# POOL's head products in halves: the order of products and masks in a four-layer kernel

## Chip, cores and metric

One core of one Trainium2 chip. The metric is the device time of one run of the whole kernel, in microseconds (us), the median of several runs.

## The reference, cut to what matters

The kernel computes four layers (an attention and a feed-forward part each) on 16 sequences of 512 tokens with 128 features. Two of the eight parts matter here.

Part 5, rotary causal attention with 16 heads of 8 features:

```python
q = _rope(proj(Wq, bq), e)
k = _rope(proj(Wk, bk), e)
v = proj(Wv, bv)
att = jnp.einsum('bhqd,bhkd->bhqk', q, k) / scale
att = jnp.where(causal[None, None], att, -jnp.inf)
att = jax.nn.softmax(att, axis=-1)
y = jnp.einsum('bhqk,bhkd->bhqd', att, v)
```

Part 8, where every token attends over its own 16 heads, before a small mixture of experts:

```python
att = jnp.einsum('bthd,btgd->bthg', q, k) / np.sqrt(HD)
att = jax.nn.softmax(att, axis=-1)
out = jnp.einsum('bthg,btgd->bthd', att, v).reshape(b, t, D)
```

For each token and each pair of heads these are 8 multiplications and a sum; POOL multiplies and VectorE sums.

## The kernel before

**Passes.** Sequences are worked on in pairs (index q, 0 or 1). A first part takes parts 1 to 4 of the reference pair by pair, then all experts of part 4 are run, then a loop of eight passes takes parts 5 to 8 (layers 4 to 7 in the code). The head attention and experts of part 8 of one pair are not done at the end of a pass: they are interleaved with part 5 and 6 of the next pass. A last part (`first == LAYERS`, once) finishes the last pair alone.

**Head products.** For a pair there are 16 products, m = 0 to 15: m 0 to 7 are phase 0 (queries by keys, four tiles of 128 tokens for each q), m 8 to 15 phase 1 (exponents by values). POOL writes product m, 128 partitions by 16 x 16 x 8 = 2,048 elements, into `ht_pr[m % 2]` (line 766), and VectorE sums over the innermost axis in two instructions of eight heads each, `take(m, 0)` and `take(m, 1)` (lines 1483 and 1486). Before product m, from m = 2 on, POOL waits for `f_read` at m - 1, which take(m - 2, 1) raises. Before take(m, half), VectorE waits for `f_pool` at m + 1.

**Part 5.** It goes over 8 quartets of heads, c = 0 to 7, each in six steps u = 0 to 5. A step has two heads and a part of the 4 x 4 tiles: steps 0 and 1 are 512 wide, 2 and 3 384, 4 and 5 256 and 128. Each engine runs its list in program order, for c from -2 to 8 and u from 0 to 5:

- TensorE: `scores_t(c, u)` (line 1909), `scores(c + 2, u)` (line 1891), then at u = 0 `values(c - 1, 1)`, at u = 1 `turn_max(c + 1)` and `values(c - 1, 2)`, at u = 3 `spread_sums(c - 1)` (line 1991), at u = 4 `values(c, 0)` (line 1932). `values(c, b)` waits for the masks of steps 2b and 2b + 1 of quartet c. Scores go round three PSUM buffers, each waiting for its reader of three turns before.
- VectorE: `maxima(c + 2, u)` on the scores (line 919), a take where `TAKE_STEP` has one, the head maxima (lines 1496 and 1497), sums (1503, 1504) or outputs (1509) at u = 1 of quartets 2 to 6 and 8, `shift(c + 1)` at u = 1 (line 943), `divide(c - 1)` at u = 5 (line 935).
- ScalarE: the exponents of `scores_t(c, u)` (line 1554), which go round five buffers.
- POOL: `mask(c, u)` on the exponents (lines 712 and 716), and between them the products: product 2 + 2c after mask (c, 1), product 3 + 2c after mask (c, 5), for c = 0 to 6. Products 0 and 1 come before quartet 0.

The takes stand at (c + 1, 0) and (c + 1, 2) for product 2 + 2c, and at (c + 1, 4) and (c + 1, 5) for product 3 + 2c. So the buffer of product 2 + 2c becomes free at VectorE's step (c, 2), that of product 3 + 2c at step (c, 5). There are two buffers.

Of the kernel before, what the change touches and what calls it, by code (L numbers as in the profile page):

```python
# [28 lines left out]
P = 128  # L29
NT = T // P  # L30
PAIR = (0, 1)
H = 16
DH = D // H
# [22 lines left out]
def program(nc, dram, x_in, out, sorted_x, sorted_y, kept_x, routes, returns, starts):  # L56
    with ExitStack() as ctx:
# [348 lines left out]
        for first, last in PARTS:  # L406
            if first == L1_EXPERTS + 1:
                sg = Signals()
# [243 lines left out]
            with nc.Fori(0, SEQS // 2 if first < LAYERS else 1) as pair:  # L652
                sg = Signals()
                with nc.Block(no_gpsimd_drain=True) as block:
# [47 lines left out]
                    def _(pool):  # L702
# [43 lines left out]
                                    if 0 <= c < QUARTETS and u % 3 == 1:  # L746
                                        send_rows(pool, sg, (2 * QUARTETS + 2 * c + u // 3,))

                        def product(m):

                            phase, q, t = m // (2 * NT), m // NT % 2, m % NT
                            if m >= 2:
                                pool.wait_ge(sg["f_read"], m - 1)
                            kv = ht_kv[q][:, t]
                            if phase == 0:
                                pr = ht_pr[m % 2].rearrange("p (h g d) -> p h g d", h=H, g=H)
                                left = ht_q[q][:, t].rearrange("p (h d) -> p h d", h=H).unsqueeze(2)
                                right = kv[:, 0:D].rearrange("p (g d) -> p g d", g=H).unsqueeze(1)
                                shape = [P, H, H, DH]
                            else:  # L760
                                pool.wait_ge(sg["f_exp"], q + 1)
                                pr = ht_pr[m % 2].rearrange("p (h d g) -> p h d g", h=H, d=DH)
                                left = ht_sc[q][:, t].unsqueeze(2)
                                right = kv[:, D:2 * D].rearrange("p (g d) -> p d g", g=H).unsqueeze(1)
                                shape = [P, H, DH, H]
                            pool.tensor_tensor(pr, left.broadcast_to(shape), right.broadcast_to(shape),  # L766
                                               ALU.mult).then_inc(sg["f_pool"], 1)

                        def finish_norms():
# [12 lines left out]
                        def l2_masks():  # L782
                            for c in range(QUARTETS):
                                for u in range(STEPS_OF):
                                    mask("l2", c, u)
                                    if u == 1 and c < HEAD_QUARTETS:
                                        product(2 + 2 * c)
                                if c < HEAD_QUARTETS:
                                    product(3 + 2 * c)

                        if first == L2_ATTENTION:
                            l2_clear()
                        if first == LAYERS:
                            for m in range(4 * NT):
                                product(m)
                            finish_norms()
                        n = 0
                        for layer in range(first, min(last, LAYERS)):
# [41 lines left out]
                            if layer == L2_ATTENTION:  # L840
                                pool.wait_ge(sg["l2_v"], len(PAIR))
                                for m in range(2):
                                    product(m)
                                l2_masks()
                            if layer == L2_ATTENTION + 1:
                                finish_norms()
# [12 lines left out]
                    def _(dve):  # L859
# [314 lines left out]
                        def l2_attention():  # L1174
# [13 lines left out]
                            def beside(c, u):  # L1188
                                if (c, u) in TAKE_STEP:
                                    take(*TAKE_STEP[c, u])  # L1190
                                if (c, u) == (2, 1):
# [285 lines left out]
                        def take(m, half):  # L1477

                            phase, q, t = m // (2 * NT), m // NT % 2, m % NT
                            dve.wait_ge(sg["f_pool"], m + 1)  # L1480
                            heads = slice(H // 2 * half, H // 2 * (half + 1))
                            if phase == 0:
                                i = dve.tensor_reduce(ht_sc[q][:, t, heads], ht_pr[m % 2].rearrange(  # L1483
                                    "p (h g d) -> p h g d", h=H, g=H)[:, heads], AX, ALU.add)
                            else:
                                i = dve.tensor_reduce(ht_o[q][:, t].rearrange("p (h d) -> p h d", h=H)[:, heads],  # L1486
                                                      ht_pr[m % 2].rearrange("p (h d g) -> p h d g", h=H, d=DH)[:, heads],
                                                      AX, ALU.add)
                            if half == 1:
                                i.then_inc(sg["f_read"], 1)  # L1490
# [1047 lines left out]
EXPERT_PAIRS = 4  # L2538
BUSY = 6
HEAD_QUARTETS = 7  # L2540
TAKE_STEP = {(-1, 1): (0, 0), (-1, 2): (0, 1), (-1, 4): (1, 0), (0, 0): (1, 1)}
for c_ in range(HEAD_QUARTETS):
    TAKE_STEP[c_ + 1, 0], TAKE_STEP[c_ + 1, 2] = (2 + 2 * c_, 0), (2 + 2 * c_, 1)
    TAKE_STEP[c_ + 1, 4], TAKE_STEP[c_ + 1, 5] = (3 + 2 * c_, 0), (3 + 2 * c_, 1)
KV_BANK = ((2, 3), (6, 7))
# [159 lines left out]
```

## Time and profile before

| | |
|---|---|
| median of 3 runs | 5653.43 us (5645.69 to 5659.54) |
| profiled execution | 5696.46 us |
| its span, first to last instruction | 5694.9 us |
| mean granted TensorE clock | 0.858 of full speed |
| instructions | 86289 |
| products on POOL (line 766) | 144: 16 in each of 8 passes and in the last part |

The profile is of one execution. A group of rows gives the busy time of the instructions of a line and the mean or median of one; a timeline row gives the start, the busy time, and in brackets how long the engine had been idle before it and which instruction released it. "x4" at the end of a timeline row means that it merges four instructions. `w_mo_wgu` in the rows is the store that holds `ht_pr`, `ht_sc` and one of the key and value buffers; `spare` and `absorbed_q` hold queries, and later outputs, of q = 0 and 1.

### The profile page before, as it was taken

The page shows a single profiled execution, that of the slowest core. Times are in us where ns is not written, and L with a number is a line of the kernel's source. Part 1 is how long each engine was busy: PE and PEld are TensorE (multiplying, and loading weights), DVE is VectorE, ACT ScalarE, POOL GpSimd, SP SyncE. Part 2 cuts the span into 40 slices and gives each one's busy share as a digit, 9 for nine tenths or more (in the row PEclk, how much of TensorE's full clock was granted, in tenths as well). Part 3 has the DMA queues.
Part 4 walks back from the last instruction along what each step waited for, and adds up shares of the span by engine and source line. Part 5 has one row for each costly group of instructions (what it writes and reads, how often), then busy time and mean ns, then how long its engine had stood idle before and what let it go on. Part 6 is the DMA issues. An engine that isn't in the chain of part 4 may idle for free. (4 is left out here: it accounts for less than half of the span.)

```text
span 5694.9 us, 86289 instructions
## 1 busy us (share of the span) xinstructions
PE 4378.5 (77%) x31912; PEld 2428.5 (43%) x31912; DVE 3661.7 (64%) x10829; ACT 1786.3 (31%) x2787; POOL 2281.8 (40%) x2766
## 2 busy tenths in 40 slices
PE   6969797888879796776778778687787886877872
PEld 4444444454535453443343443434443434344341
DVE  4565656565556565458677686685776866768765
ACT  2424242423333323333224232332232422423230
POOL 3333332323333333556336244372362533624435
PEclk9989898989989898887878888888788888888885
DMA  3000000000000001760000000000000000000000
GB/s 122 11 15 16 9 16 9 16 9 16 9 16 10 15 10 57 226 188 14 14 16 7 17 10 9 14 9 17 14 6 18 9 10 17 9 17 11 9 14 4
DMA packets 143893, 147.30 MB, mean 26 GB/s; under 512 B 31180, under 2 KB 128142, under 8 KB 142926
## 3 DMA queue, kind: packets, MB, share of 16 engines
q1 hardware_dynamic: 116286, 94.67, 5.6%
q0 software_dynamic: 18432, 37.79, 2.3%
q10 hardware_dynamic: 8736, 8.91, 0.5%
q8 instruction: 285, 4.67, 0.3%
q14 instruction: 154, 1.26, 0.1%
HBM read 70.83 MB, written 63.11 MB: 24 GB/s over the span
## 5 line engine op out<-in xcount | busy, mean ns | idle before, releaser
L919 DVE CUSTOM_DVE_ANT_0 twin<-twin,w_mask_row 128x512 f32<-128x512 f32 (+3 forms) x2048 | 950.9, 520 | 333.1 <-PE twin L1891 331.4
L1891 PE MATMUL twin<-arena 32*128 32x128 f32 (+3 forms) x4096 | 809.4, 522 | 37.0 <-DVE arena L919 16.9
L1909 PE MATMUL twin<-arena 32*128 32x128 f32 (+3 forms) x4096 | 795.9, 507 | 31.1 <-DVE arena L919 29.7
L1554 ACT ACTIVATE arena<-twin 128x768 f32<-128x768 f32 (+1 forms) x544 | 478.9, 880 | 674.4 <-PE twin L1920 387.9
L1909 PEld LDWEIGHTS twin<-arena 32*128 32x128 f32 x4096 | 351.9, 202 | 482.0 <-issue 293.6
L827 POOL TENSOR_SCALAR ve<-mv 128x4 f32<-128x4 f32 x128 | 27.5, 215 | 1158.2 <-DVE mv L879 1157.5
L377 POOL DMA_INDIRECT got<-sorted_y,back x288 | 278.1, 966 | 495.7 <-ACT ring L1758 306.2
L1836 PE MATMUL twin<-w_ident_b 128*128 128x512 bf16 x1200 | 344.5, 438 | 132.3 <-DVE mv L879 50.3
L1891 PEld LDWEIGHTS twin<-arena 32*128 32x128 f32 x4096 | 361.0, 208 | 196.2 <-issue 109.0
L369 POOL DMA_INDIRECT sorted_x<-got,w_mo_first_slots x288 | 284.1, 986 | 139.7 <-issue 65.5
L1932 PE MATMUL twin<-arena 128*32 128x128 f32 (+3 forms) x2944 | 304.1, 457 | 9.0 <-POOL arena L712 9.0
L919 DVE DVE_READ_ACCUMULATOR2_ANT arena<- 128x1 f32 x2048 | 288.8, 141 | 0.0
L712 POOL TENSOR_SCALAR_AFFINE_SELECT arena<-arena 128x256 f32<-128x256 f32 x352 | 144.7, 413 | 345.0 <-ACT arena L1554 344.5
L1554 ACT ACTIVATE ring<-twin 128x768 f32<-128x768 f32 (+1 forms) x224 | 194.9, 878 | 218.8 <-PE twin L1909 216.9
L1836 PEld LDWEIGHTS twin<-w_ident_b 128*128 128x128 bf16 x1200 | 121.2, 110 | 330.6 <-DVE mv L879 69.5
L833 POOL TENSOR_TENSOR rs<-ve,minus_half 128x4 f32<-128x4 f32 x208 | 223.3, 1073 | 17.3
L766 POOL TENSOR_TENSOR w_mo_wgu<-w_mo_wgu,w_l_cs_feat 128x2048 f32<-128x2048 f32 x36 | 197.4, 5488 | 52.5 <-DVE w_mo_wgu L1483 25.6
L1932 PE MATMUL twin<-ring,arena 128*32 128x384 f32 (+3 forms) x1152 | 163.1, 525 | 57.3 <-POOL ring L712 50.0
L766 POOL TENSOR_TENSOR w_mo_wgu<-w_mo_wgu 128x2048 f32<-128x2048 f32 x36 | 197.7, 5495 | 20.0 <-DVE spare L1486 14.1
L766 POOL TENSOR_TENSOR w_mo_wgu<-spare,w_l_cs_feat 128x2048 f32<-128x2048 f32 x36 | 161.4, 4495 | 88.8 <-DVE arena L1183 85.9
L716 POOL TENSOR_SCALAR_AFFINE_SELECT arena<-arena 128x512 f32<-128x512 f32 x192 | 123.8, 650 | 160.0 <-ACT arena L1554 159.9
L1483 DVE TENSOR_REDUCE w_mo_wgu<-w_mo_wgu 128x128 f32<-128x1024 f32 x144 | 174.1, 1214 | 20.8 <-POOL w_mo_wgu L766 20.8
(440 smaller groups left out, 9392.6 us busy)
## 6 DMA issues: line engine op xcount, KB each, us to landing
sorted_y<-arena SPq DMA_DIRECT2D x96, 256.0 KB, 2.8
sorted_x<-zeros ACTq DMA_DIRECT2D x2, 4096.0 KB, 20.0
a<-sorted_x SPq DMA_DIRECT2D x64, 128.0 KB, 2.5
b<-sorted_x SPq DMA_DIRECT2D x64, 128.0 KB, 3.0
hres<-sorted_x SPq DMA_DIRECT2D x64, 128.0 KB, 2.5
x<-x_in SPq DMA_DIRECT2D x18, 256.0 KB, 3.4
sorted_x<-got,w_mo_first_slots POOLq DMA_INDIRECT x288
x_next<-kept_x SPq DMA_DIRECT2D x18, 256.0 KB, 2.8
```

Of the source, the lines that this page charges most:

```text
L369: pool.indirect_dma_start(sorted_x[r % GROUPS], bass.IndirectOffsetOnAxis(ap=slot_of[:, q, n:n + 1], axis=0), normed[q][:, r // GROUPS], N ...
L377: pool.indirect_dma_start(got[q][:, n], None, sorted_y, bass.IndirectOffsetOnAxis(ap=back[:, q, n:n + 1].bitcast(U32), axis=0)).then_inc(s ...
L712: pool.affine_select(p, p, [[0, 2], [1, P]], ALU.is_ge, 0.0, base=0, channel_multiplier=-1).then_inc(sg[tag + "_masked"], 1)
L766: pool.tensor_tensor(pr, left.broadcast_to(shape), right.broadcast_to(shape), ALU.mult).then_inc(sg["f_pool"], 1)
L833: pool.tensor_tensor(RS[q][:], VE[q][:], minus_half[:], ALU.pow).then_inc(sg["rstd_ready"], 1)
L919: last = dve.tensor_tensor_reduce(s[:, e, at:at + w], s[:, e, at:at + w], W["mask_row"][:, T - w:T], -1.0, 3e38, ALU.add, ALU.min, into)
L1483: i = dve.tensor_reduce(ht_sc[q][:, t, heads], ht_pr[m % 2].rearrange("p (h g d) -> p h g d", h=H, g=H)[:, heads], AX, ALU.add)
L1554: act.activation(at_pt[tag][n % len(at_pt[tag])][:, :, 0:w], twin[SLOT["scores_t", c, u] % 3][:, :, 0:w], ACT.Exp, scale=1.0 if tag == "l1 ...
L1836: pe.matmul(into, ident_b, ident_b.unsqueeze(1).broadcast_to([P, NT, P]), start=True, stop=True, skip_group_check=True)
L1891: last = pe.matmul(s[:, e, at:at + w], queries[r, P * i:P * (i + 1)], keys[r, 0:w], start=(at == 0), stop=True, skip_group_check=True)
L1909: last = pe.matmul(s[:, e, at:at + w], keys[r, P * m:P * (m + 1)], queries[r, P * m:T], start=(at == 0), stop=(tag == "l2"), skip_group_ch ...
L1932: last = pe.matmul(bank[into][rows_of(j), P * m:T], weights(m, j), at_pt[tag][n % len(at_pt[tag])][:, j % 2, at:at + w], start=(m == 0), s ...
```

## The change

Each product becomes two instructions of eight heads, 1,024 elements each, both behind the same wait for `f_read`, and each raises `f_pool`. A take waits for its own half. In part 5 the four halves of a quartet stand behind the masks of steps 0, 1, 3 and 5 (`HALF_AT`), where the two whole products stood behind those of steps 1 and 5. In the last part, and for products 0 and 1, the two halves follow each other.

```diff
-                        def product(m):
+                        def product(m, half):
                             phase, q, t = m // (2 * NT), m // NT % 2, m % NT
+                            heads = slice(H // 2 * half, H // 2 * (half + 1))
                             if m >= 2:
                                 pool.wait_ge(sg["f_read"], m - 1)
...
-                                shape = [P, H, H, DH]
+                                shape = [P, H // 2, H, DH]
...
-                            pool.tensor_tensor(pr, left.broadcast_to(shape), right.broadcast_to(shape),
+                            pool.tensor_tensor(pr[:, heads], left[:, heads].broadcast_to(shape), right.broadcast_to(shape),
                                                ALU.mult).then_inc(sg["f_pool"], 1)
...
                                 for u in range(STEPS_OF):
                                     mask("l2", c, u)
-                                    if u == 1 and c < HEAD_QUARTETS:
-                                        product(2 + 2 * c)
-                                if c < HEAD_QUARTETS:
-                                    product(3 + 2 * c)
+                                    if c < HEAD_QUARTETS and u in HALF_AT:
+                                        which, half = divmod(HALF_AT.index(u), 2)
+                                        product(2 + 2 * c + which, half)
...
-                            dve.wait_ge(sg["f_pool"], m + 1)
+                            dve.wait_ge(sg["f_pool"], 2 * m + half + 1)
...
+HALF_AT = (0, 1, 3, 5)
```

## Rows read from the trace of the kernel before

**Rows 1.** The page: busy time of each engine over the span

```profile
PE 4378.5 (77%) x31912; PEld 2428.5 (43%) x31912; DVE 3661.7 (64%) x10829; ACT 1786.3 (31%) x2787; POOL 2281.8 (40%) x2766
```

**Rows 2.** Timeline of POOL, first pass, last pass: start, us, [idle before, releaser]

```profile
2635.16 4.52 POOL L766 TENSOR_TENSOR w_mo_wgu<-absorbed_q,w_mo_wgu 128x2048 f32<-128x2048 f32 x1 [1.93 <-DVE w_mo_wgu L1483]
...
2645.99 0.80 POOL L712 TENSOR_SCALAR_AFFINE_SELECT ring<-ring 128x256 f32<-128x256 f32 x2
2650.76 4.51 POOL L766 TENSOR_TENSOR w_mo_wgu<-absorbed_q,w_mo_wgu 128x2048 f32<-128x2048 f32 x1 [3.97 <-DVE w_mo_wgu L1483]
...
2655.94 0.65 POOL L716 TENSOR_SCALAR_AFFINE_SELECT arena<-arena 128x512 f32<-128x512 f32 x1
...
2657.14 4.54 POOL L766 TENSOR_TENSOR w_mo_wgu<-absorbed_q,w_mo_wgu 128x2048 f32<-128x2048 f32 x1
...
2665.87 5.44 POOL L766 TENSOR_TENSOR w_mo_wgu<-w_mo_wgu,w_l_cs_feat 128x2048 f32<-128x2048 f32 x1 [3.47 <-DVE w_mo_wgu L1483]
...
2682.55 5.47 POOL L766 TENSOR_TENSOR w_mo_wgu<-w_mo_wgu,w_l_cs_feat 128x2048 f32<-128x2048 f32 x1 [2.18 <-DVE spare L1486]
...
2697.51 5.46 POOL L766 TENSOR_TENSOR w_mo_wgu<-w_mo_wgu 128x2048 f32<-128x2048 f32 x1 [1.42 <-DVE spare L1486]
...
2719.92 5.49 POOL L766 TENSOR_TENSOR w_mo_wgu<-w_mo_wgu 128x2048 f32<-128x2048 f32 x1
...
5238.23 4.51 POOL L766 TENSOR_TENSOR w_mo_wgu<-absorbed_q,w_mo_wgu 128x2048 f32<-128x2048 f32 x1 [1.93 <-DVE w_mo_wgu L1483]
...
5300.05 5.43 POOL L766 TENSOR_TENSOR w_mo_wgu<-w_mo_wgu 128x2048 f32<-128x2048 f32 x1 [1.22 <-DVE spare L1486]
```

**Rows 3.** Timeline of VectorE, first pass

```profile
2640.11 1.21 DVE L1483 TENSOR_REDUCE w_mo_wgu<-w_mo_wgu 128x128 f32<-128x1024 f32 x1
...
2646.73 1.23 DVE L1497 TENSOR_TENSOR w_mo_wgu<-w_mo_wgu 128x1024 f32<-128x1024 f32 x1
...
2649.46 1.22 DVE L1483 TENSOR_REDUCE w_mo_wgu<-w_mo_wgu 128x128 f32<-128x1024 f32 x1
...
2652.19 0.43 DVE L919 CUSTOM_DVE_ANT_0 twin<-twin,w_mask_row 128x256 f32<-128x256 f32 x1 [0.47 <-PE twin L1891]
...
2654.55 0.42 DVE L919 CUSTOM_DVE_ANT_0 twin<-twin,w_mask_row 128x256 f32<-128x256 f32 x1
...
2655.77 1.21 DVE L1483 TENSOR_REDUCE w_mo_wgu<-w_mo_wgu 128x128 f32<-128x1024 f32 x1
...
2664.57 1.21 DVE L1483 TENSOR_REDUCE w_mo_wgu<-w_mo_wgu 128x128 f32<-128x1024 f32 x1
...
2670.30 1.22 DVE L1483 TENSOR_REDUCE w_mo_wgu<-w_mo_wgu 128x128 f32<-128x1024 f32 x1
...
2704.82 6.00 DVE L1509 TENSOR_TENSOR spare<-spare,w_mo_wgu 128x512 f32<-128x512 f32 x1
```

**Rows 4.** Timeline of TensorE, first pass

```profile
2652.01 1.19 PE L1932 MATMUL twin<-ring,arena 128*32 128x512 f32 x8
2653.13 0.48 PE L1909 MATMUL twin<-arena 32*128 32x256 f32 x2
...
2665.67 1.07 PE L1932 MATMUL twin<-ring,arena 128*32 128x512 f32 x8
...
2672.09 0.86 PE L1932 MATMUL twin<-arena 128*32 128x384 f32 x8 [2.15 <-POOL arena L712]
...
2703.76 1.51 PE L1932 MATMUL twin<-ring,arena 128*32 128x384 f32 x8 [2.57 <-POOL ring L712]
```

**Rows 5.** Line 1932, all passes: TensorE's idle time until this row's instruction: us, times

```profile
  POOL ring L712: 125.3, 61
```

**Rows 6.** Timeline of POOL in layer 0: a 1,024-element product

```profile
61.00 2.37 POOL L802 TENSOR_TENSOR w_mo_wgu<-w_mo_wgu,w_l_cs_feat 128x1024 f32<-128x1024 f32 x1
```

**Rows 7.** Line 1509 over the span: min/median/max ns

```profile
L1509 DVE TENSOR_TENSOR spare<-spare,w_mo_wgu x9: 674/5552/6011, 2704.8 to 5625.4; 128x512 f32<-128x512 f32 x9
```

**Rows 8.** Windows, quartet 5: PE, PEld, DVE, ACT, POOL busy, clock, DMA share, GB/s

```profile
2697.50:2712.50 15.00, 11.81 (x86) 4.71 (x86) 15.00 (x28) 6.78 (x9) 13.94 (x8) 0.77 0.00 1
```

More of the change, by code:

```diff
@@ L764, in product @@
                                 right = kv[:, D:2 * D].rearrange("p (g d) -> p d g", g=H).unsqueeze(1)
-                                shape = [P, H, DH, H]
-                            pool.tensor_tensor(pr, left.broadcast_to(shape), right.broadcast_to(shape),
+                                shape = [P, H // 2, DH, H]
+                            pool.tensor_tensor(pr[:, heads], left[:, heads].broadcast_to(shape), right.broadcast_to(shape),
                                                ALU.mult).then_inc(sg["f_pool"], 1)
@@ L794, in _ @@
                             for m in range(4 * NT):
-                                product(m)
+                                product(m, 0)
+                                product(m, 1)
                             finish_norms()
@@ L842, in _ @@
                                 for m in range(2):
-                                    product(m)
+                                    product(m, 0)
+                                    product(m, 1)
                                 l2_masks()
```

## The prediction

> **What bounds the kernel now.** I read the page first [rows 1]: TensorE is busy 77% of the span, VectorE 64%, POOL 40%. No engine is full on average, so the stage has to be looked at alone. The change touches one stage: the attention of layer 4 with the head products of the last layer interleaved into it, once in each of eight passes, and again the products alone in the last part. There I read the timelines of POOL, VectorE and TensorE side by side, with quartets c and steps u as in the kernel section. Write T(c) for the end of the reduction (the "take") at step (c, 2), U(c) for the end of the one at step (c, 5).
>
> The reader is to see three things. VectorE runs almost without a gap: from T(2) = 2650.68 to T(3) = 2665.78 its one gap is 0.47 us, before the maxima at 2652.19 [rows 3]. POOL has room, but not in every place: product 2+2c starts 0.08 us after T(c), having waited 3.97, 3.47, 2.18 and 1.42 us for it [rows 2]. Both masks (c, 0) and (c, 1) had been made before that wait (the pair at 2645.99) [rows 2]. And TensorE takes the masked tiles in program order: `values` (c, 0) at 2652.01 in quartet 2 and at 2665.67 in quartet 3, thus 1.3 us after T(2) and 0.1 us before T(3), without an idle bracket, since its masks were long there. Where POOL's long product does stand in TensorE's way is `values` (c, 1): 2.15 and 2.57 us idle until the mask, 125.3 us over all passes [rows 4, 5].
>
> **What the change does, part by part.** The buffer a product writes is free at the same event as before: its wait is `f_read` at m - 1, which the second half of a take raises. So half products don't start earlier than T(c) and U(c). What moves is what is queued behind the wait on POOL. Product (2+2c, 0) now stands ahead of mask (c, 1), and product (3+2c, 0) ahead of masks (c, 4) and (c, 5). The masks now wait for T(c), or U(c), and then for a half product. POOL sends no DMA here and SP's queue isn't passed.
>
> Price of a half: the trace has a 128x1024 product of POOL, 2.37 us [rows 6], against 4.51 for 2,048 elements [rows 2], so halving leaves about 0.12 us behind on each half. For the slower form of phase 1 I take 5.46 / 2 + 0.1 = 2.83. (Lower bound: exactly half, 2.25 and 2.73.)
>
> **New first part, T(c) to U(c).** 0.08 until the half starts, 2.37 the half, 0.40 the mask (c, 1), 0.06 to TensorE, 1.12 `values` (c, 0) (2652.01 to 2653.13), 0.95 the two score groups of step 5 (2653.13 to 2654.08), 0.12 to VectorE, 1.22 its maxima (2654.55 to 2655.77), 1.21 the take: 7.53 us, in phase 1 (c from 3) 7.99. Before it was 6.30 in quartet 2 (2650.68 to 2656.98) and 5.74 in quartet 3 (2665.78 to 2671.52) [rows 2, 3, 4]. TensorE had been ahead of VectorE by only 0.5 us in quartet 2 (scores done 2654.08, maxima at 2654.55), so this is not swallowed.
>
> **New second part, U(c) to T(c+1).** POOL: half, masks (c, 4) and (c, 5) (0.65 + 0.60), then the other half. TensorE gets mask (c, 5) at U + 3.7 to 4.2 and has the scores of step (c+1, 2) done 1.8 us later, at U + 6; VectorE comes to them only at U + 6.6 or later. So this part stays VectorE's own: 8.80 us after an even quartet (2656.98 to 2665.78) and 9.36 after an odd one (2641.32 to 2650.68) [rows 3]. One thing is added. The DVE product 128x1024 of line 1497 begins 5.41 us after U(1) (2646.73), and in the new order POOL's other half then runs, until U + 6.07 in phase 0 and U + 6.99 in phase 1. The trace shows what comes of that: line 1509, the same kind of instruction on 128x512, took 6.00 us at 2704.82 (POOL's product 13 began at the same moment), with a median of 5.55 against a least of 0.67 [rows 3, 7]. It was held until POOL's instruction ended. That would add 0.66 us in quartet 1 and 1.58 in quartet 3.
>
> That row has a rule in the Trainium skill, page "SBUF — State Buffer", section "Who interferes with whom": a DVE instruction with two inputs in SBUF and a GpSimd one that reads SBUF share a read port, and whichever starts first holds it to its end. The trace agrees (6.00 us for what takes 0.67 alone). By itself the rule speaks for the change: shorter POOL instructions hold VectorE for less.
>
> **Sum of a pass.** T(1) to T(5): quartet 1: 7.53 + 9.36 + 0.66 = 17.55; 2: 7.53 + 8.80 = 16.33; 3: 7.99 + 9.36 + 1.58 = 18.93; 4: 7.99 + 8.80 = 16.79; together 69.6 us. Before: 62.35 (2635.16 to 2697.51), in the last pass 61.82 [rows 2], over the eight passes 61.82 to 63.86 with mean 62.7. So +6.9. Quartet 0 has no wait for a take on these products and is left as it is.
> Tail, from T(5) on: VectorE has no maxima after quartet 5 and POOL alone paces. New: 7.99 to U(5), 0.08, then six halves (13 to 15) of 2.83 and masks of 0.4 + 0.4 + 0.8 + 1.25 + 1.25 = 4.1: 29.15 us. Before: 2697.51 to 2725.41, 27.9 [rows 2]; over the passes 26.7 to 27.95, mean 27.4. So +1.7. The held head output (6.00 us) gets shorter, but POOL's 1.2 us wait behind it was already all that it cost. What follows the tail (masks and values of quartet 7, the outputs) is serial and moves along.
> Together +8.6 us a pass. Whether line 1497 is really held depends on a phase of one or two us, so I count half of the 2.24: +7.5, times eight +60. In the last part 16 products run back to back on POOL (four in 21.79 us): 32 halves cost some 0.1 us more each product, +1.6, and two takes overlap a half, -2.4: -1. **+59 us.**
>
> The profiled execution took 5696.46 us (span 5694.9), the median of the runs is 5653.43, 43 below; its stages are taken as those of any run, so I add the same 59 to the median: **5712 us**.
>
> Bounds. Low: halves at exactly half (8 on the path and 6 in the tail, -1.6 a pass) and line 1497 never held (-2.24): +4.75 a pass, 38 - 1 = +37, 5690. High: line 1497 held in full (8.6) and TensorE's clock low. The windows of quartet 5 show 0.77 granted, and after 2.57 us idle the eight 384-wide matmuls took 1.51 us where they had taken 0.86 in quartet 3: towards the lower of the two levels, 1.2 GHz, after an idle wait [rows 4, 8]. The new order makes a wait of 2 to 3 us ahead of `values` (c, 0). At the low clock the 1.12 + 0.95 cost 1.85 more, in four quartets 7.4: 16 us a pass, +128, 5781.
>
> The Trainium skill says, in "TensorE: Matmul & The Clock Gate", section "Part 1: The HAM clock gate", that an idle engine falls to 1.2 GHz and must be busy again to get 2.4. The trace shows both levels in this very stage; by that rule the sum goes towards its upper bound.
>
> **Rivals.**
> *Faster.* Product and mask finely interleaved: `values` (c, 1) no longer waits (2.15 us in quartet 3), the head output is held for half as long. What VectorE could get back is U(3) to T(4), 10.95 us against the 9.36 of its own work = 1.6, about 0.5 in quartet 4, and POOL's 1.2 in the tail: 3.3 a pass, -26: 5627. It decides if mask (c, 1) isn't late, that is if TensorE arrives at `values` (c, 0) more than 2.9 us after T(c). It arrived 1.3 after and 0.1 before, so I give it little.
> *No change.* TensorE's delay lies in VectorE's shadow and only the tail's overhead stays: 5650 to 5665. It needs scores ready over 2 us before their maxima at step 5; they were 0.5 us ahead.
> *Clock.* As the upper bound: TensorE low in most quartets, 5781 or a little above.
>
> **How the numbers follow.** Forecast (5685 to 5755) 0.60; clock and other additions above it 0.11; a smaller loss, 5670 to 5685, 0.09; no change 0.10; faster 0.10. The 0.3% that a measurement of this kernel can tell from no change is 17 us. Slower 0.80, same 0.10, faster 0.10. For 8 in 10 the range reaches down to 5648 and up to 5780; the likeliest case's own range is 5685 to 5755.
>
> **What would show it.** Right: TensorE's idle until a mask moves from `values` (c, 1) to `values` (c, 0), 2 to 3 us each; T(1) to T(5) grows to about 69 us; VectorE idles 1 to 2 us before the maxima of step 5; half products at 2.3 to 2.4 and 2.8 us; line 1509 falls below 4 us and line 1497 rises above 1.23. Wrong: TensorE reaches `values` (c, 0) later than I think, or VectorE's gap is filled by work it had put off; then the quartets keep their 15 to 17 us.

## The result and the profile after

The changed kernel takes 5752.97 us (median of 4 runs, 5747.67 to 5753.94), the kernel before 5651.65 us on the same chip (4 runs): ratio 1.0178, 95% interval 1.0159 to 1.0197, or 101 us slower. The profiled execution took 5752.96 us, its span 5751.4 us, mean clock 0.855.

The page of the changed kernel, busy time and VectorE's maxima (last column: VectorE's idle time ahead of the group and what ended it):

```profile
PE 4380.7 (76%) x31912; PEld 2422.8 (42%) x31912; DVE 3664.8 (64%) x10829; ACT 1784.6 (31%) x2787; POOL 2318.1 (40%) x2910
...
L921 DVE CUSTOM_DVE_ANT_0 twin<-twin,w_mask_row 128x512 f32<-128x512 f32 (+3 forms) x2048 | 950.2, 519 | 422.2 <-PE twin L1893 421.0
```

VectorE and TensorE are busy as long as before, POOL 36.3 us longer for 144 more instructions [rows 1]. So nearly all of the loss is waiting, and the page already says where: VectorE waits 421 us for scores of line 1893 (that group had 331.4 us in the page of before). The timelines show how. POOL, quartets 2 and 3 of the first pass:

```profile
2599.82 2.33 POOL L767 TENSOR_TENSOR w_mo_wgu<-absorbed_q,w_mo_wgu 128x1024 f32<-128x1024 f32 x1 [2.54 <-DVE w_mo_wgu L1485]
2602.10 0.40 POOL L712 TENSOR_SCALAR_AFFINE_SELECT ring<-ring 128x256 f32<-128x256 f32 x1
2602.48 2.34 POOL L767 TENSOR_TENSOR w_mo_wgu<-absorbed_q,w_mo_wgu 128x1024 f32<-128x1024 f32 x1
...
2617.08 2.79 POOL L767 TENSOR_TENSOR w_mo_wgu<-w_mo_wgu,w_l_cs_feat 128x1024 f32<-128x1024 f32 x1 [2.59 <-DVE w_mo_wgu L1485]
2619.81 0.42 POOL L712 TENSOR_SCALAR_AFFINE_SELECT ring<-ring 128x256 f32<-128x256 f32 x1
2620.19 2.84 POOL L767 TENSOR_TENSOR w_mo_wgu<-w_mo_wgu,w_l_cs_feat 128x1024 f32<-128x1024 f32 x1
...
2626.41 2.82 POOL L767 TENSOR_TENSOR w_mo_wgu<-w_mo_wgu,w_l_cs_feat 128x1024 f32<-128x1024 f32 x1 [2.65 <-DVE w_mo_wgu L1485]
```

TensorE, the same places:

```profile
2602.55 1.48 PE L1934 MATMUL twin<-ring,arena 128*32 128x512 f32 x8 [2.87 <-POOL ring L712]
...
2620.28 1.94 PE L1934 MATMUL twin<-ring,arena 128*32 128x512 f32 x8 [2.95 <-POOL ring L712]
2622.15 0.80 PE L1911 MATMUL twin<-arena 32*128 32x256 f32 x2
```

And VectorE:

```profile
2619.17 1.21 DVE L1485 TENSOR_REDUCE w_mo_wgu<-w_mo_wgu 128x128 f32<-128x1024 f32 x1
2623.88 0.43 DVE L921 CUSTOM_DVE_ANT_0 twin<-twin,w_mask_row 128x256 f32<-128x256 f32 x1 [3.50 <-PE twin L1893]
...
2625.11 1.21 DVE L1485 TENSOR_REDUCE w_mo_wgu<-w_mo_wgu 128x128 f32<-128x1024 f32 x1
```

The reader is to follow one round. POOL waits for the take that frees the buffer until 2617.08. Mask (3, 1) is queued behind that half product: it is done at 2620.23. TensorE has waited 2.95 us for it and begins `values` (3, 0) at 2620.28. The scores of step 5 are queued behind `values`, so VectorE idles 3.50 us before its maxima at 2623.88, and only then comes the next take, whose end at 2626.32 frees the buffer for the next product at 2626.41. In the kernel before, the same `values` had no idle bracket [rows 4], and VectorE's one gap in a quartet was 0.47 us [rows 3].

All waits of TensorE's matmuls of line 1934 for a mask, over the eight passes (us, times):

```profile
  POOL ring L712: 74.9, 41
  POOL arena L716: 54.3, 24
  POOL ring L716: 37.2, 23
  POOL arena L712: 31.0, 14
```

Together 197.4 us, against 65.7 us in the kernel before, 50.0 of it in the first group. The 125.3 us of [rows 5] is larger because that view adds the idle time ahead of the weight loads of the same line, which is largely the same time: it would count a wait twice.

For the rest I use one measure for all kernels, read from the starts of the products in the POOL timeline: T(1) to T(5) is the time from the start of product 4 to that of product 12, the tail from there to the end of product 15, the pass is from product 0 to the end of product 15 (means over eight passes); "last part" is the same from product 0 to the end of product 15 there. With more than two buffers a product no longer starts at the end of a take, and there only the column "pass" compares. "Masks" is the sum of the matmuls' waits as above. "Held" is the time by which VectorE's 16 subtractions of the head maxima (two in each pass, line 1499, 1.23 us when nothing holds them) took longer than that. All but the ratio is read from the one profiled execution of each kernel.

| kernel | ratio to before, 95% | T(1) to T(5) | tail | pass | last part | masks | held |
|---|---|---|---|---|---|---|---|
| before | 1 | 62.70 | 27.46 | 130.3 | 85.54 | 65.7 | 6.8 |
| changed | 1.0178 (1.0159 to 1.0197) | 72.71 | 29.19 | 142.0 | 90.96 | 197.4 | 13.7 |
| split only | 0.999 (0.997 to 1.001) | 63.27 | 27.26 | 131.3 | 86.68 | 85.9 | 12.3 |
| whole early | 1.0524 (1.0496 to 1.0552) | 91.3 | 31.1 | 161.9 | 85.53 | 277.7 | 2.3 |
| early first | 1.0153 (1.0132 to 1.0174) | 72.62 | 28.94 | 142.4 | 86.76 | 136.2 | 0.7 |
| early second | 1.0069 (1.0051 to 1.0088) | 64.58 | 28.13 | 132.5 | 90.98 | 130.1 | 12.1 |
| filled | 1.0171 (1.0132 to 1.0211) | 68.83 | 29.97 | 138.3 | 86.72 | 139.5 | 13.8 |
| three buffers | 0.9983 (0.9968 to 0.9998) | 64.17 | 29.0 | 128.5 | 91.02 | 33.1 | 29.2 |
| three buffers, whole | 1.005 (1.0036 to 1.0063) | 68.6 | 28.62 | 134.3 | 85.59 | 23.6 | 58.8 |
| four buffers | 1.0047 (1.0027 to 1.0067) | 65.54 | 29.75 | 130.9 | 86.18 | 26.9 | 44.0 |
| four buffers, whole | 1.009 (1.0071 to 1.0108) | 67.25 | 27.03 | 133.2 | 85.06 | 23.6 | 57.0 |
| before, no subtraction | 0.995 (0.993 to 0.9969) | 58.68 | 27.91 | 127.4 | 83.25 | 82.9 | - |
| changed, no subtraction | 1.0119 (1.0102 to 1.0136) | 67.33 | 29.48 | 137.7 | 84.46 | 169.1 | - |
| four, no subtraction | 0.9851 (0.9831 to 0.9872) | 54.01 | 30.32 | 119.3 | 83.96 | 17.5 | - |

A pass grew by 11.7 us: 8 x 11.7 = 93.6, and 5.4 in the last part, 99 us. This is not quite the whole: from the start of the first product to the end of the span the trace of the changed kernel is 109 us longer than that of before (3208.2 against 3099.2). Some 11 us lie between the passes (241.5 us from a product 15 to the next product 0, against 240.1), a stretch that wasn't followed; without whole early, the other kernels have 239.0 to 242.1 there. The medians differ by 101, so a sum from these two traces is good to some 10 us. The runs stood on several chips, and the median of the kernel before was 5645 to 5652 us on some and 5689 to 5693 on others, a difference that lies ahead of the eight passes. That is why ratios are taken within a chip, and why the profile of before (5696.46 us) stands 43 us above its median: its first product starts at 2595.7, that of the changed kernel at 2543.2.

### The profile page after: what moved, and what is told of

Read it like the earlier page. It is cut to its first block and busy times, and to the rows that moved or that the text cites. A ratio compares the mean times of both kernels' runs of the same rounds, so it can differ in the third digit from the quotient of the medians.

```text
span 5751.4 us, 86505 instructions
## 1 busy us (share of the span) xinstructions
PE 4380.7 (76%) x31912; PEld 2422.8 (42%) x31912; DVE 3664.8 (64%) x10829; ACT 1784.6 (31%) x2787; POOL 2318.1 (40%) x2910
## 5 line engine op out<-in xcount | busy, mean ns | idle before, releaser
L1893 PE MATMUL twin<-arena 32*128 32x128 f32 (+3 forms) x4096 | 837.4, 537 | 42.5 <-DVE arena L921 18.9
L1911 PE MATMUL twin<-arena 32*128 32x128 f32 (+3 forms) x4096 | 810.3, 521 | 7.9 <-DVE arena L921 6.7
L1911 PEld LDWEIGHTS twin<-arena 32*128 32x128 f32 x4096 | 365.8, 209 | 454.6 <-issue 307.2
L1893 PEld LDWEIGHTS twin<-arena 32*128 32x128 f32 x4096 | 370.0, 213 | 219.2 <-issue 106.2
L1934 PE MATMUL twin<-arena 128*32 128x128 f32 (+3 forms) x2944 | 317.1, 467 | 85.3 <-POOL arena L716 54.3
L767 POOL TENSOR_TENSOR w_mo_wgu<-w_mo_wgu,w_l_cs_feat 128x1024 f32<-128x1024 f32 x72 | 203.5, 2830 | 88.0 <-DVE w_mo_wgu L1485 46.6
L767 POOL TENSOR_TENSOR w_mo_wgu<-w_mo_wgu 128x1024 f32<-128x1024 f32 x72 | 202.5, 2817 | 32.8 <-DVE spare L1488 28.1
L767 POOL TENSOR_TENSOR w_mo_wgu<-absorbed_q,w_mo_wgu 128x1024 f32<-128x1024 f32 x72 | 168.6, 2347 | 89.6 <-DVE w_mo_wgu L1485 89.6
L767 POOL TENSOR_TENSOR w_mo_wgu<-spare,w_l_cs_feat 128x1024 f32<-128x1024 f32 x72 | 166.8, 2334 | 87.4 <-DVE arena L1185 84.5
```

What stands on the lines that cost most here:

```text
L767: pool.tensor_tensor(pr[:, heads], left[:, heads].broadcast_to(shape), right.broadcast_to(shape), ALU.mult).then_inc(sg["f_pool"], 1)
L1893: last = pe.matmul(s[:, e, at:at + w], queries[r, P * i:P * (i + 1)], keys[r, 0:w], start=(at == 0), stop=True, skip_group_check=True)
L1911: last = pe.matmul(s[:, e, at:at + w], keys[r, P * m:P * (m + 1)], queries[r, P * m:T], start=(at == 0), stop=(tag == "l2"), skip_group_ch ...
L1934: last = pe.matmul(bank[into][rows_of(j), P * m:T], weights(m, j), at_pt[tag][n % len(at_pt[tag])][:, j % 2, at:at + w], start=(m == 0), s ...
```

## The experiments

**1. Split only.** The changed kernel, with the halves where the whole products had been.

```diff
-                                    if c < HEAD_QUARTETS and u in HALF_AT:
-                                        which, half = divmod(HALF_AT.index(u), 2)
-                                        product(2 + 2 * c + which, half)
+                                    for n, behind in enumerate(HALF_AT if c < HEAD_QUARTETS else ()):
+                                        if behind == u:
+                                            product(2 + 2 * c + n // 2, n % 2)
-HALF_AT = (0, 1, 3, 5)
+HALF_AT = (1, 1, 5, 5)
```

> Halves as in the changed kernel, but back in the places of the whole products: both halves of product 2+2c behind mask (c, 1), both of 3+2c behind mask (c, 5). Queue theory (the loss comes from masks that stand behind the wait for the buffer): T(1) to T(5) back to 62 to 64 us a pass, the overhead of 0.1 us a half shows only in the tail (+0.6 a pass) and a shorter hold of the head output gives up to 1.2 back; in all 5640 to 5665. Rival (the splitting itself costs, by 144 more POOL instructions, counts and holds of VectorE): 5700 or more.

Measured: 5640.99 us against 5644.58, ratio 0.999 (0.997 to 1.001). The 144 added instructions cost nothing that can be told. The loss is in the places.

**2. Whole early.** The kernel before, with its whole products behind steps 0 and 3.

```diff
-                                    if u == 1 and c < HEAD_QUARTETS:
+                                    if u == 0 and c < HEAD_QUARTETS:
                                         product(2 + 2 * c)
-                                if c < HEAD_QUARTETS:
-                                    product(3 + 2 * c)
+                                    if u == 3 and c < HEAD_QUARTETS:
+                                        product(3 + 2 * c)
```

> The kernel before with whole products, but product 2+2c behind mask (c, 0) and 3+2c behind mask (c, 3): the places of the first halves of the change. Queue theory: mask (c, 1) now waits for T(c) and a whole product, 2.2 to 2.7 us longer than in the changed kernel, and masks (c, 4) and (c, 5) put the values (c, 2) past VectorE's own pace by 1.5 to 2: T(1) to T(5) about 88 us, the kernel 5840 to 5910. Rival (splitting itself costs): close to the kernel before, 5650 to 5680.

Measured: 5945.29 us, ratio 1.0524, T(1) to T(5) 91.3 us, both above what I had written (about 88 us, 5840 to 5910). With the whole product ahead of the masks the chain is a half product longer still. In the first pass TensorE waits 2.34 to 4.45 us ahead of the `values` (c, 0) of quartets 1 to 5.

**3. Three buffers.** The changed kernel with a third product buffer, so that product m waits for the takes of m - 3.

```diff
+        ht_pr.append(got[0][:].rearrange("p n d -> p (n d)"))
...
-                            if m >= 2:
-                                pool.wait_ge(sg["f_read"], m - 1)
+                            if m >= 3:
+                                pool.wait_ge(sg["f_read"], m - 2)
...
-                                pr = ht_pr[m % 2].rearrange("p (h g d) -> p h g d", h=H, g=H)
+                                pr = ht_pr[m % 3].rearrange("p (h g d) -> p h g d", h=H, g=H)
```

> The changed kernel with a third product buffer (in the store of the fetched rows, unused in this stage), so that a half product waits for the take of three products before and finds it done. Order of masks and halves unchanged. Queue theory with the wait for the buffer as its cause: POOL's waits for takes are gone, mask (c, 1) comes about 2.8 us after mask (c, 0) at most, T(1) to T(5) 59 to 63 us a pass, the kernel 5610 to 5655. If instead the fine interleaving as such is at fault (more POOL work ahead of a mask), it stays above 5700.

Measured: 5638.58 us, ratio 0.9983 (0.9968 to 0.9998); a pass takes 128.5 us against 142.0. The order of POOL's queue is that of the change, only the wait at its head is for an earlier take, and the whole loss is gone: TensorE's waits for masks fall from 197.4 to 33.1 us. It is the fastest full kernel of this study, 0.2% below the kernel before, just clear of no difference. T(1) to T(5) is 64.17 us, above the 59 to 63 that I had expected; VectorE's holds, which grow here, stand with experiment 12.

**4. Filled.** The changed kernel, in which TensorE does eight matmuls of 512 columns that nobody reads, in the time in which it would wait for mask (c, 1). They change its activity and nothing that others wait for.

```diff
-                                pe.wait_ge(sg[tag + "_masked"], STEPS_OF * c + 2 * b + 2)
                                 if b == 0 and c >= 1:
                                     pe.wait_ge(sg["l1_y" if tag == "l1" else "l2_taken"], c)
+                                if tag == "l2" and b == 0 and 1 <= c < HEAD_QUARTETS:
+                                    for _ in range(FILL):
+                                        pe.matmul(bank[6], ident_b, ident_b.unsqueeze(1).broadcast_to([P, NT, P]),
+                                                  start=True, stop=True, skip_group_check=True)
+                                pe.wait_ge(sg[tag + "_masked"], STEPS_OF * c + 2 * b + 2)
...
+FILL = 8
```

> The changed kernel with eight bf16 matmuls of 512 columns (results overwritten) in front of values (c, 0), c = 1 to 6, where TensorE idles for 3 us. The mask's wait stays as it is. If the low TensorE clock makes the part that my sum missed (about 1.2 us in quartets 2 to 5), values (c, 0) falls from 1.94 to about 1.1 us, U - T from 9.3 to 8.0 to 8.3, the kernel by 25 to 40 us to 5713 to 5728. If the clock doesn't matter, the time stays at 5753 or rises, as the fill may outlast the wait.

TensorE of this kernel in quartet 3 of the first pass, to be held beside the rows at 2620.28 above:

```profile
2618.61 1.90 PE L1962 MATMUL twin<-w_ident_b 128*128 128x512 bf16 x8
2621.66 1.07 PE L1934 MATMUL twin<-ring,arena 128*32 128x512 f32 x8 [1.15 <-POOL ring L712]
2622.66 0.48 PE L1911 MATMUL twin<-arena 32*128 32x256 f32 x2
```

Its VectorE, the maxima behind them:

```profile
2623.72 0.43 DVE L921 CUSTOM_DVE_ANT_0 twin<-twin,w_mask_row 128x256 f32<-128x256 f32 x1 [1.99 <-PE twin L1893]
```

Windows of the first pass, product 4 to the end of product 15 (PE, PEld, DVE, ACT and POOL busy, clock, DMA share, GB/s), of this kernel:

```profile
2582.70:2685.00 102.30, 82.99 (x612) 33.70 (x612) 81.28 (x199) 43.08 (x56) 80.29 (x59) 0.91 0.00 1
```

and of the changed kernel, then of its quartets 2, 4 and 5 alone:

```profile
2582.70:2685.60 102.90, 76.29 (x559) 31.19 (x558) 79.05 (x193) 41.88 (x54) 81.26 (x60) 0.83 0.00 1
...
2599.80:2617.10 17.30, 12.61 (x102) 5.49 (x102) 14.58 (x41) 6.51 (x9) 11.96 (x11) 0.90 0.00 1
2637.10:2655.30 18.20, 13.04 (x92) 5.19 (x86) 14.56 (x40) 7.31 (x9) 13.81 (x10) 0.78 0.00 0
2655.30:2672.50 17.20, 13.41 (x89) 5.38 (x88) 12.98 (x29) 5.74 (x8) 14.63 (x11) 0.70 0.01 2
```

The same eight matmuls of `values` (3, 0) take 1.07 us with the fill and 1.94 without, 1.07 before [rows 4]; VectorE's gap falls from 3.50 to 1.99 us, T(1) to T(5) from 72.71 to 68.83 us, and the granted clock of the stretch rises from 0.83 to 0.91 (0.89 in the kernel before). The time of the run did not follow beyond doubt: the median was 5736.83 us, ratio 1.0171 (1.0132 to 1.0211), where I had expected 5713 to 5728, and this profiled execution was the fastest of its four, 5707.91 us. What the clock is worth in a pass is thus read from one execution. The four differ in clock as well: those of 5707.91 and 5722.91 us had a mean granted clock of 0.870 and 0.867, those of 5750.75 and 5759.42 us had 0.857 and 0.856, near the 0.852 to 0.855 of the changed kernel. So only two of the four had a higher clock with the fill, and why isn't known. The Trainium skill says in "TensorE: Matmul & The Clock Gate", section "Part 1: The HAM clock gate", that the throttled clock is the default and that activity releases it. This case agrees: activity alone, with nothing done sooner by it, gave 1.07 for 1.94 us.

**5 and 6. Early first, early second.** Only the first, or only the second product's halves where the change puts them. The loop is that of experiment 1.

```diff
-HALF_AT = (0, 1, 3, 5)
+HALF_AT = (0, 1, 5, 5)
```

and for the second

```diff
-HALF_AT = (0, 1, 3, 5)
+HALF_AT = (1, 1, 3, 5)
```

> Halves, with only the first product of a quartet moved forward: product (2+2c, 0) behind mask (c, 0), its other half behind mask (c, 1); both halves of product 3+2c behind mask (c, 5). My point by point account puts the whole loss in this place (the part from T(c) to U(c)): T(1) to T(5) 70 to 73 us a pass, the kernel 65 to 100 us above before, 5710 to 5745. Rival (the delay of masks (c, 4) and (c, 5) is what costs): within 20 us of before.

> Halves, with only the second product moved forward: both halves of product 2+2c behind mask (c, 1), product (3+2c, 0) behind mask (c, 3), its other half behind mask (c, 5). By my account values (c, 2) then wait for masks that come 3.7 to 4.2 us after U(c), but VectorE gets to the scores behind them later still: T(1) to T(5) 63 to 65 us, the kernel within 20 us of before, 5630 to 5665, with a TensorE wait at the values (c, 2) in the trace that costs nothing. Rival: 30 to 60 us slower.

Measured: early first 5777.38 us against 5692.79, ratio 1.0153, a pass 12.1 us longer: as much as in the whole change, and with almost no hold of the subtraction (0.7 us in all). Early second 5725.1 us, ratio 1.0069: 32 us by the medians, 39 by the ratio, outside what I had expected (at most 20). Of these, 8 x 2.2 = 18 us are in the passes and 5.4 in the last part of the profiled execution; some 9 lie between the passes (241.2 us against 240.1), and what they are wasn't followed. Its waits for masks are 130.1 us, nearly those of early first (136.2), and they cost 2.2 us a pass where those cost 12.1: a mask that is late behind U(c) is late in VectorE's shadow, one behind T(c) isn't.

**7 and 8. Four buffers, four buffers whole.** The changed kernel and the kernel before with four product buffers; both edits are as in experiment 3 with 4 for 3.

```diff
+        ht_pr += [got[q][:].rearrange("p n d -> p (n d)") for q in PAIR]
...
+                            if m >= 4:
+                                pool.wait_ge(sg["f_read"], m - 3)
```

> The changed kernel with four product buffers (both stores of fetched rows), so that no half product waits for a take any more; with three, product 3+2c still waited for T(c) and masks (c, 4) and (c, 5) behind it. If the wait for the buffer is the whole cause, POOL never idles for a take, T(1) to T(5) 59 to 63 us and the kernel is 15 to 35 us faster than before, 5610 to 5630. If POOL's work ahead of the masks is a cause of its own, it stays like the three buffers, about 5635.

> The kernel before (whole products in their old places) with four product buffers. Tells what the buffers alone give: POOL no longer idles 1.2 to 4 us before product 2+2c, so masks (c, 2) and (c, 3) come earlier and values (c, 1) don't wait 2 us. If the change's fine spreading has a value of its own once the wait is gone, four_buffers beats this one by 5 us or more; if not, both are the same at 5610 to 5640.

Measured: 5723.57 and 5732.15 us against 5692.79. Both missed: I had expected them below the kernel before, and they are above it, 1.0047 and 1.009. The halves beat the whole products by 9 us, as expected. TensorE's waits for masks are down to 26.9 and 23.6 us, so something else came in. POOL of four buffers, first pass:

```profile
2648.40 2.37 POOL L768 TENSOR_TENSOR got<-absorbed_q,w_mo_wgu 128x1024 f32<-128x1024 f32 x1
2650.68 0.45 POOL L713 TENSOR_SCALAR_AFFINE_SELECT ring<-ring 128x256 f32<-128x256 f32 x1
2651.05 0.45 POOL L713 TENSOR_SCALAR_AFFINE_SELECT arena<-arena 128x256 f32<-128x256 f32 x1
2651.43 2.37 POOL L768 TENSOR_TENSOR got<-absorbed_q,w_mo_wgu 128x1024 f32<-128x1024 f32 x1
2660.13 0.64 POOL L717 TENSOR_SCALAR_AFFINE_SELECT arena<-arena 128x512 f32<-128x512 f32 x1 [6.34 <-ACT arena L1557]
```

VectorE, the same time:

```profile
2648.63 1.21 DVE L1499 TENSOR_REDUCE w_mo_wgu<-w_mo_wgu 128x64 f32<-128x1024 f32 x1
2649.88 5.00 DVE L1500 TENSOR_TENSOR w_mo_wgu<-w_mo_wgu 128x1024 f32<-128x1024 f32 x1
2654.80 0.67 DVE L946 TENSOR_TENSOR arena<-arena,twin 128x512 f32<-128x512 f32 x1
```

The subtraction of the head maxima (two inputs in SBUF, 1.23 us alone) began during a product and ended at 2654.88, over the end of that product, two masks and a whole second product, 1.1 us after POOL had gone idle at 2653.80, which is about its own duration. The first subtraction of each of the eight passes went this way (4.97 to 5.00 us); the second was let in sooner, at the end of a half or shortly behind it (2.63 to 3.74 us). In the changed kernel every hold of a subtraction ended with the half that it had met. VectorE, which bounds the stage, stands meanwhile. The median of these instructions is 4356 ns in four buffers, 4471 in four buffers whole, against 1240 before and 2088 in the changed kernel.

**9 to 11. Without the subtraction.** To measure that, the subtraction is left out in three kernels.

```diff
-                            done(dve.tensor_reduce(red, sc, AX, ALU.max))
-                            dve.tensor_tensor(sc, sc, red.unsqueeze(2).broadcast_to([P, NT * H, H]),
-                                              ALU.subtract).then_inc(sg["f_sc"], 1)
+                            dve.tensor_reduce(red, sc, AX, ALU.max).then_inc(sg["f_sc"], 1)
```

> The kernel before without the subtraction of the head maxima (line 1497, 128x1024, both inputs in SBUF; the exponents are then taken unshifted). It was held by POOL in few passes, so leaving it out saves its own 1.23 us twice a pass where VectorE paces: 10 to 20 us faster than before.

> The changed kernel without the same subtraction. Its hold by POOL's other half was 0.4 and 1.3 us in a pass. If that is the share of the loss that I gave it, this kernel is 14 us closer to its own reference point than before_nosub: 1.2 + 1.7 us a pass less, 25 to 35 us below the changed kernel, and still some 1.2 to 1.5% above before. If the hold is the whole of the loss, it falls to the time of before.

> Four product buffers, halves in the places of the change, without the subtraction. With four buffers POOL runs its products and masks back to back and the subtraction took 4.4 us in the median (up to 5.0) for 1.23. If the hold is what ate the gain of the fourth buffer: 2 times 4.4 us a pass come back, 50 to 75 us below four_buffers, 0.5 to 1% below before and clearly below before_nosub. If something else ate it (POOL's work ahead of the masks), it gains only the 10 to 20 us that before_nosub gains.

Measured: 0.995, 1.0119 and 0.9851. Without it the kernel before wins 0.5 points (28 us, more than the 10 to 20 that I had written), the changed kernel 0.59 points (33 us), that with four buffers 1.96 points (some 110 us, above my 50 to 75). So the hold's share in the loss of the change is about 5 us and can't be told from none; in four buffers the subtraction cost some 110 - 28 = 80 us more than it does in the kernel before, and was what had eaten the gain: without it this kernel is 1.0% faster than the kernel before with the same edit. Of the 80 us the rows show 44.0 - 6.8 = 37 as hold. Where the other half comes from wasn't followed.

**12. Three buffers whole.** The kernel before with the edit of experiment 3.

> The kernel before with a third product buffer, whole products in their old places. Product 2+2c then waits for U(c-1), long past, product 3+2c for T(c). Against three_buffers (0.998 of before): if the spreading in halves is what made that one faster, this is at 1.000 or above; if the third buffer alone did, the same 0.998. With holds of the subtraction by whole products (up to 5.5 us) I expect 1.000 to 1.006.

Measured: 5719.58 us against 5688.84, ratio 1.005 (1.0036 to 1.0063). A third buffer alone is a loss; with the change's order it is none. Halves between masks are thus worth 0.7 points (1.005 against 0.9983) once the wait at their head is gone; whether by the split or by the places, no run tells apart.

The traces point at VectorE's holds. With a third buffer and whole products the 16 subtractions are held for 58.8 us in all (each took 3.85 to 6.17 us), in the kernel before for 6.8; the run is 31 us longer. With halves the holds are 29.2 us. TensorE's waits for masks are no reason: 23.6 us, lower than in the kernel before. This kernel without the subtraction wasn't run, so the cause is argued from rows and not shown.

## Why the prediction was right, and where its sum was short

The forecast was 5712 us, +59; measured was 5752.97, +101, inside the range (5648 to 5780) and just inside the likeliest case's own, which ended at 5755. The mechanism stands; the first part of a round was priced too low, and a term for the last part held in some executions only. This is about them.

**Same start, other queue: right.** Splitting alone does nothing (experiment 1); a third buffer, which moves the wait and not the order, takes the whole loss back (3). Half products of the first pass took 2.33 to 2.38 and 2.79 to 2.86 us (2.37 and 2.83 predicted). The 125.3 us that the prediction gives for TensorE's waits ahead of `values` (c, 1) count weight loads and matmuls both; the matmuls alone waited 50.0 us. The sum didn't use that figure.

**First part, T(c) to U(c): the mechanism right, the size too small.** Predicted 7.53 in phase 0 and 7.99 in phase 1; measured in the first pass 7.3 and 8.5 in quartets 1 and 2 (phase 0), then 9.3, 9.15 and 9.2 in quartets 3 to 5 (phase 1). In quartet 3 the chain is the predicted one link by link to TensorE's start: half from 2617.08 (2.79), mask (0.42), `values` at 2620.28. Then `values` took 1.94 us instead of 1.12, the scores behind it were later by a further 0.6, and VectorE idled 3.50 us, not 1 to 2. I had put TensorE's clock among the rivals with 0.11 and its price at 7.4 us a pass. In the profiled execution with the fill it is 3.9 of the 10.0 us that T(1) to T(5) grew by; the other 6.1 are the queue, for which I had 6.9 less half of the hold, 5.8. In the windows above the granted clock was 0.90 in quartet 2, 0.78 in quartet 4 and 0.70 in quartet 5, where it had been 0.77 [rows 8]. This is the term that failed in the passes: a wait that the change itself brings, once every quartet, lowers the clock of what stands behind it. By how much the run's time would be lower at full clock is less certain than the 3.9, since the four runs of experiment 4 spread over 50 us. The likeliest case's sum had no clock in it, and the result lies only 2 us inside the upper end of that case's range.

**Second part, U(c) to T(c + 1): right.** Predicted 8.80 behind an even quartet, 9.36 behind an odd one, with up to 1.58 for a held subtraction: 10.94 in quartet 3. Measured 8.79, 10.70 and 9.08 in quartets 2, 3 and 4. Experiment 6 shows the same from the other side: the halves behind steps 3 and 5 alone add 2.2 us a pass.

**The held subtraction: half right.** The rows of the 16 subtractions and of the 8 head outputs in the passes of the changed kernel (min/median/max ns):

```profile
L1499 DVE TENSOR_TENSOR w_mo_wgu<-w_mo_wgu x16: 1603/2088/2574, 2595.4 to 5327.2; 128x1024 f32<-128x1024 f32 x16
...
L1511 DVE TENSOR_TENSOR spare<-spare,w_mo_wgu x8: 1791/1802/1810, 2666.1 to 5358.5; 128x512 f32<-128x512 f32 x8
```

Held it was, twice in every pass, for 0.4 us in quartet 1 and 1.3 in quartet 3 (0.66 and 1.58 predicted), and in the passes the head output fell below 4 us as predicted [rows 7]. But in the kernel before the subtraction was held too (up to 2.96 us), so the difference is small: 13.7 us in all against 6.8 by the rows, and 5 us of the 101 by experiments 9 and 10. The passes of early first grow as much as those of the whole change with no hold to speak of.

**Tail: right.** Predicted +1.7, measured 29.19 - 27.46 = +1.73; U(5) to the end of product 15 in the first pass 21.04 us, predicted 21.1.

**Last part: -1 predicted, +5.4 measured in this execution.** VectorE and POOL of the changed kernel there:

```profile
5676.99 10.13 DVE L1511 TENSOR_TENSOR spare<-spare,w_mo_wgu 128x512 f32<-128x512 f32 x1
```

```profile
5675.66 10.92 POOL L767 TENSOR_TENSOR w_mo_wgu<-w_mo_wgu 128x1024 f32<-128x1024 f32 x4
5691.30 10.95 POOL L767 TENSOR_TENSOR w_mo_wgu<-w_mo_wgu 128x1024 f32<-128x1024 f32 x4 [4.72 <-DVE absorbed_q L1488]
```

The head output (0.68 us alone, 3.45 in this place before) was held over the rest of the first half and the three behind it, 10.13 us. The takes behind it came late, POOL ran out of free buffers and waited 4.72 us: that wait is nearly the 5.4. I had priced only the instructions and assumed that a hold ends with the half it met.

Of the 5.4 us, 4 are not the change's own. Split only, early first and filled have the same last part, instruction by instruction. In their profiled executions the same head output was let in behind the first half, took 1.98 to 2.00 us, and the last part took 86.7 to 86.8 us, 1.2 more than before. Only early second shows the long hold once more (10.14 us, last part 90.98). How often the changed kernel's runs have it isn't on record.

**Sum.** Predicted 7.5 a pass, measured 11.7; in the passes +93.6 instead of +60, in the last part +5.4 instead of -1: 33.6 + 6.4 = 40 of the 41 us between forecast and result. That this comes out to 1 us is luck: the traces differ by 109 us where the medians differ by 101, and some 4 of the 6.4 belong to a hold that sister kernels don't have.

**The rivals.** Faster and no change fell: TensorE had reached `values` (c, 0) 2.87 and 2.95 us before mask (c, 1) was done in quartets 2 and 3, that is within 0.3 us of T(c), and "faster" needed it 2.9 us after T(c) or later. The clock was no rival but a part of the whole, and would have belonged in the sum.

Open stays: some 10 us between the passes of the changed kernel and of early second; whether holds are why whole products lose by a third buffer; how often the long hold of the last part occurs; and what the changed kernel's run time would be at a full clock.

## What to carry to other kernels

Before moving a long instruction forward in an in-order queue, look at what stands at its head: if the wait is for a buffer, the instruction doesn't start sooner, and everything that it is moved past now starts later, by the wait and by the instruction. Ask first for another buffer, and only then for another order; here neither helped alone, both together gave 0.2%, and a fourth buffer lost again, because POOL's work now held VectorE's. And where a change makes TensorE wait once per turn, put the matmuls behind the wait into the sum at the lower clock.

## What the runs showed of the hardware that was not expected

**A held VectorE instruction is let in between two of POOL's in some places and not in others.** Where POOL's instructions follow each other without a gap, a VectorE instruction with two inputs in SBUF can stay held over several of them: 5.00 us over the end of a half, two masks and another half (four buffers), 10.13 us over four halves (changed kernel), and in three buffers 15.60 us over six, from 5555.73 to 5571.33. Its VectorE and its POOL:

```profile
5555.73 15.60 DVE L1512 TENSOR_TENSOR spare<-spare,w_mo_wgu 128x512 f32<-128x512 f32 x1
```

```profile
5554.36 10.96 POOL L768 TENSOR_TENSOR w_mo_wgu<-w_mo_wgu 128x1024 f32<-128x1024 f32 x4
5565.24 5.54 POOL L768 TENSOR_TENSOR got<-w_mo_wgu 128x1024 f32<-128x1024 f32 x2
```

POOL's six halves end at 5570.78, and VectorE's instruction 0.55 us later.

In other places it went on at the first border. All 16 subtractions and all 8 head outputs in the passes of the changed kernel did. VectorE and POOL, the subtraction of quartet 3:

```profile
2631.73 2.57 DVE L1499 TENSOR_TENSOR w_mo_wgu<-w_mo_wgu 128x1024 f32<-128x1024 f32 x1
```

```profile
2630.38 2.84 POOL L767 TENSOR_TENSOR w_mo_wgu<-w_mo_wgu,w_l_cs_feat 128x1024 f32<-128x1024 f32 x1
2633.16 1.41 POOL L712 TENSOR_SCALAR_AFFINE_SELECT ring<-ring 128x256 f32<-128x256 f32 x1
```

The half ends at 2633.22, the subtraction 1.08 us later, and this time the mask behind the half took 1.41 us where its kind takes 0.40: now POOL was the one that stood. The head output went the same way:

```profile
2666.13 1.79 DVE L1511 TENSOR_TENSOR spare<-spare,w_mo_wgu 128x512 f32<-128x512 f32 x1
```

```profile
2664.57 2.80 POOL L767 TENSOR_TENSOR w_mo_wgu<-w_mo_wgu 128x1024 f32<-128x1024 f32 x1 [2.53 <-DVE spare L1488]
2667.33 1.08 POOL L716 TENSOR_SCALAR_AFFINE_SELECT ring<-ring 128x512 f32<-128x512 f32 x1
2668.37 0.63 POOL L716 TENSOR_SCALAR_AFFINE_SELECT arena<-arena 128x512 f32<-128x512 f32 x1
```

It ended at 2667.92, 0.55 us after the product, and the mask took 0.45 us more than the next of its kind.

A border between two products can do as well. In the last part of split only the head output took 1.98 us, while POOL ran eight halves without a gap:

```profile
5570.57 1.98 DVE L1511 TENSOR_TENSOR spare<-spare,w_mo_wgu 128x512 f32<-128x512 f32 x1
```

It began 1.34 us after the start of a half. In the changed kernel, at the same place in the same order of instructions, it began 1.33 us after it and was held for four. What decides between the two wasn't tried. So halves of a product can shorten a hold (2.57 us at most for the changed kernel's subtractions, 3.85 to 6.17 with three buffers and whole products), but one can't count on it.

The Trainium skill says in "SBUF — State Buffer", section "Who interferes with whom", that the engine that starts first has the shared port for its whole instruction and the other is blocked. Who is held agrees in the rows shown here. Who comes next, when POOL's instructions follow without a gap, is not settled by that: in the rows of 5.00, 10.13 and 15.60 us it was POOL again, in those of 2.57, 1.79 and 1.98 us VectorE.
